# A gate computed inside an attention, and scatters issued beside it

## The reference

```python
x = x + attention(layernorm(x), ctx, mask)          # 16 heads of 16, 77 keys
xn = layernorm(x)
scores = softmax(xn @ Wg)                           # Wg 256 x 32, 32 experts
weights, indices = top_k(scores, 4)
for e in range(32):                                 # capacity 2048 pairs each
    tok, w = the pairs that chose e, in order
    y[tok] += swiglu(xn[tok], W1[e], W2[e], W3[e]) * w
x = x + y + swiglu(xn, Ws1, Ws2, Ws3)               # shared expert, width 256
x = x + attention(layernorm(x), ctx)
x = x + ffn(layernorm(x))                           # weights of +1 and -1
```

## Time and profile before

| | |
|---|---|
| three runs | 1355.96 us median, 1355.4 to 1363.51 |
| the profiled execution | 1356.17 us; its span in the trace 1354.4 us |
| granted TensorE clock, mean | 0.933 |
| PE / DVE / ACT / POOL busy | 87% / 57% / 38% / 30% of the span |

### The profile page before, as it was taken

One profiled execution on the slowest core, in us unless ns is written; L12 is line 12 of the kernel. 1 busy time (PEld: TensorE's weight loads), 2 busy tenths in 40 slices (PEclk: granted clock), 3 DMA queues, 4 the chain that ended last, 5 costly groups with the idle time before them and its releaser, 6 DMA issues. The chain is left out here.

```text
span 1354.4 us, 26011 instructions
## 1 busy us (share of the span) xinstructions
PE 1172.3 (87%) x8528; PEld 810.8 (60%) x8528; DVE 765.4 (57%) x2032; ACT 512.3 (38%) x1049; POOL 409.5 (30%) x495
## 2 busy tenths in 40 slices
PE   7699999677682399999999448899989999999998
PEld 4378888445441277778877323788865555555554
DVE  4177778565562156666656495788873434244331
ACT  6555555222230034443433136566642222222221
POOL 5260000466575445555555344600000000000000
PEclk9899999787786799999999768899999999999999
DMA  9199100263162554445444291000000000000000
GB/s 176 24 308 392 49 2 2 82 102 95 66 216 101 190 163 148 148 147 180 152 136 118 90 371 51 14 2 2 1 2 1 16 16 17 0 15 15 16 16 16
DMA packets 100754, 123.94 MB, mean 92 GB/s; under 512 B 33984, under 2 KB 76051, under 8 KB 100631
## 3 DMA queue, kind: packets, MB, share of 16 engines
q1 hardware_dynamic: 86807, 87.98, 22.1%
q0 software_dynamic: 13824, 34.38, 7.1%
HBM read 61.78 MB, written 64.72 MB: 93 GB/s over the span
## 5 line engine op out<-in xcount | busy, mean ns | idle before, releaser
L1847 PE MATMUL psA<-H,B 128*128 128x512 f16 x1024 | 223.5, 379 | 0.0
L1774 DVE SCALAR_TENSOR_TENSOR H<-psA,H 128x512 f16<-128x512 f32 x128 | 88.3, 690 | 208.3 <-ACT H L1815 208.3
L1533 POOL DMA_INDIRECT y_rows<-YB,pair x160 | 155.5, 972 | 149.0 <-DVE YB L1588 80.9
L1815 ACT ACTIVATE H<-psA 128x512 f16<-128x512 f32 x128 | 76.4, 597 | 252.7 <-PE psA L1847 252.7
L1847 PEld LDWEIGHTS psA<-H,B 128*128 128x128 f16 x1024 | 100.2, 98 | 119.3
L1643 PE MATMUL psH<-W,XT 128*128 x640 | 168.1, 386 | 0.5 <-ACT XT L1545 0.4
L203 POOL TENSOR_SCALAR var<-mv 128x4 f32<-128x4 f32 x32 | 13.7, 429 | 508.2 <-DVE mv L197 507.1
L1206 POOL DMA_INDIRECT x_rows<-XN,slot_s x128 | 130.6, 1021 | 71.5 <-issue 43.9
L806 DVE TENSOR_TENSOR PLT<-psT,PHT 128x512 f16<-128x512 f32 (+1 forms) x192 | 113.9, 595 | 38.8 <-ACT PHT L857 38.3
L857 ACT ACTIVATE PHT<-psT 128x512 f16<-128x512 f32 (+1 forms) x192 | 94.4, 525 | 102.4 <-PE psT L916 102.4
L1643 PEld LDWEIGHTS psH<-W,XT 128*128 128x128 f32 x640 | 110.1, 192 | 12.0 <-issue 3.1
(11 more groups left out here) (249 smaller groups left out, 2039.0 us busy)
## 6 DMA issues: line engine op xcount, KB each, us to landing
XG<-x_rows SPq DMA_DIRECT2D x160, 134.0 KB
y_rows<-zero_row SPq DMA_DIRECT2D x4, 4096.0 KB, 27.5
G<-y_rows SPq DMA_DIRECT2D x7, 2048.0 KB, 10.3
x_rows<-zero_row SPq DMA_DIRECT2D x33, 134.0 KB, 8.7
X<-in_x SPq DMA_DIRECT2D x8, 512.0 KB, 7.2
QT<-in_w SPq DMA_DIRECT2D x1, 4096.0 KB
out_x<-OUT SPq DMA_DIRECT2D x8, 512.0 KB
y_rows<-YB,pair POOLq DMA_INDIRECT x160
```

The lines of the kernel that those rows point to most:

```text
L1533: pool.indirect_dma_start(y_rows[:, :], bass.IndirectOffsetOnAxis(ap=pair[u // HALF][:, u % HALF:u % HALF + 1], axis=0), YB[u][:], None, b ...
L1774: dve.scalar_tensor_tensor(out=H[layer][1][:, o], in0=psA[k % 4][:], scalar=0.0, in1=H[layer][0][:, o], op0=ALU.max, op1=ALU.subtract).the ...
L1847: last = pe.matmul(psA[k % 4][:], W[:, c, o * P:(o + 1) * P], src[part][:, c], start=n == 0, stop=n == 2 * n_in - 1)
```

## The change

A class `Gate` takes the place of `Chosen`, `RouteTail` and the gate code of route. Its steps are called from `body(t)` of the first attention, each at a slot `t = K + 4 m`: transposes at K = 8, logits at 9, pick and index at 11, mark at 12, ranks at 13, place and slots at 14; ACT's `apply` at 7 writes the normalized rows straight into the row buffers (before: DVE L210, then ACT L1370). The statistics of one tile are at the end of each body. `mark` is one comparison and two bf16 additions where there was a reduction (L1010). Six macros are gated there, a seventh is transposed there, and 70 of the 128 scatters are issued there: all 16 of macros 0 to 3, and 6 of macro 4. In route remain the gates of macros 6 and 7 (bodies 0 and 1) and 58 scatters; plan, second keys and values are at other bodies, w1 comes in attention, and W2 in 16 pieces of 256 KB behind the `up`s.

```diff
-ROWBUFS = 2
+ROWBUFS = 4
+GATED_EARLY, SCATTERED_EARLY, TURNED_EARLY = 6, 4, 7
+CUT = 6
+TURN_AT, LOGITS_AT, PICK_AT, RANKS_AT, SCATTER_AT = 8, 9, 11, 13, 15
+KEYS_AT = 1
 # attend, gpsimd
+                    for m in range(SCATTERED_EARLY):
+                        gate.scatter(pool, m, 0, MT * TOPK)
+                        gate.power(pool, m + MT - 1)
+                    gate.scatter(pool, SCATTERED_EARLY, 0, CUT)
 # attend, vector: body(t)
+                    if gate:
+                        for m in gate.due(t, RANKS_AT + 1, GATED_EARLY):
+                            dve.wait_ge(gate.c_done, m + 1)
                     if ok(t - 2):
                         norm(t - 2, u)
+                    if gate:
+                        gate_reads(t)
                     if ok(t + 1):
                         maximum(t + 1, 1 - u, 0)
...
+                    if gate:
+                        gate_steps(t)
 # attend, scalar: end of body(t)
...
+                        for m in gate.due(t, LOGITS_AT + 1, GATED_EARLY):
+                            gate.exps(act, m)
+                        for h in range(2):
+                            for m in gate.due(t, TURN_AT, TURNED_EARLY):
+                                gate.turned_out(act, m, h, rows_piece(m, h))
+                            for m in gate.due(t, TURN_AT - 1, TURNED_EARLY):
+                                gate.apply(act, m, h)
+                        for m in gate.due(t, PICK_AT + 1, GATED_EARLY):
+                            gate.tops(act, m)
 # attend, tensor: body(t)
+                        for m in gate.due(t, TURN_AT, TURNED_EARLY):
+                            for h in range(2):
+                                bank_free(pe, (gate, m, h))
+                                gate.turn(pe, m, h, rows_piece(m, h))
+                        for m in gate.due(t, RANKS_AT + 1, GATED_EARLY):
+                            pe.wait_ge(gate.ranks_read, m + 1)
                     if ok(t - 1):
                         values(t - 1, 1 - u)
...
+                        for m in gate.due(t, RANKS_AT, GATED_EARLY):
+                            gate.ranks(pe, m)
+                        for m in gate.due(t, LOGITS_AT, GATED_EARLY):
+                            bank_free(pe, (gate, m, "logits"))
+                            gate.logits(pe, m, logits_piece(m))
 # Gate
+        def recycled(self, eng, m):
+            if m >= ROWBUFS:
+                eng.wait_ge(self.scattered[m % ROWBUFS], SCATTERS * (m // ROWBUFS))
...
+        def mark(self, dve, m):
...
+            self.own.done(dve.tensor_tensor(self.two, self.hot[:, :, 0:2, :], self.hot[:, :, 2:4, :], ALU.add))
+            dve.tensor_tensor(self.chosen, self.two[:, :, 0, :], self.two[:, :, 1, :], ALU.add).then_inc(self.chosen_s, 1)
 # route, sync
-                load_down(sp)
+                def down(m):
+                    sp.wait_ge(h_done, (m + 1) * 2 * KC)
+                    load_down(sp, 2 * m, 2)
+                    load_down(sp, EXPERTS // 2 + 2 * m, 2)
 # route, tensor
+                for b in range(MACROS):
+                    if b < PLAN_AT:
...
+                        gate.logits(pe, GATED[b], psL)
+                    up(b, 0)
+                    if b:
+                        shared_out(b - 1)
...
+                    up(b, 1)
...
```

More of the change, by code:

```diff
@@ L745, in ok @@
             return not isinstance(t, int) or 0 <= t < TILES
+        TURNS = []
+        for t in range(TILES + 3):
+            TURNS += [(t, g) for g in range(NG) if t < TILES]
+            if gate:
+                TURNS += [(gate, m, h) for m in gate.due(t, TURN_AT, TURNED_EARLY) for h in range(2)]
+                TURNS += [(gate, m, "logits") for m in gate.due(t, LOGITS_AT, GATED_EARLY)]
+        ORDER = {key: i for i, key in enumerate(TURNS)}
         def steady(body, beside):
@@ L1189, in _ @@
                         sp.dma_start(x_rows[ds(row, P), :], zero_row[:, 0:ROW]).then_inc(tails_st, 16)
+                for m in range(PLAN_AT, MACROS):
+                    down(m)
                 sp.wait_ge(tails_st, 16 * EXPERTS)
@@ L1211, in _ @@
-                for m in range(MACROS):
-                    body(m, m % ROWBUFS)
+                kv.blanks(pool)
+                gate.power(pool, MACROS - 1)
+                for m in range(SCATTERED_EARLY, MACROS):
+                    first = CUT if m == SCATTERED_EARLY else 0
+                    gate.scatter(pool, m, first, MT * TOPK)
                 for b in range(ROWBUFS):
-                    pool.wait_ge(scattered[b], SCATTERS * len(range(b, MACROS, ROWBUFS)))
+                    pool.wait_ge(gate.scattered[b], SCATTERS * len(range(b, MACROS, ROWBUFS)))
@@ new lines, in silu, with rest_out @@
+                    act.activation(SG[:, o], psH[bank(m, o, 0)][:], ACT.Silu).then_inc(silu_s, 1)
+                def rest_out(m):
+                    act.wait_ge(gate.turned, 2 * m + 2)
+                    act.activation(QT[:, :, m * MW:(m + 1) * MW], psX[:], ACT.Copy).then_inc(gate.xt_out, 2)
+                for m in range(TURNED_EARLY, MACROS):
+                    for h in range(2):
+                        gate.apply(act, m, h)
+                for b in range(MACROS):
+                    if b < PLAN_AT:
+                        gate.exps(act, GATED[b])
+                    silu(b, 0)
+                    if b < PLAN_AT:
+                        gate.tops(act, GATED[b])
+                    if b == KEYS_AT:
@@ L1464, in body @@
                                   stop=True).then_inc(plan_spread, 1)
-                    if m:
-                        shared_out(m - 1)
-                    if m + 2 < MACROS:
-                        turn_in(m + 2, u)
-                        logits(m + 2, u)
-                pe.sem_inc(turned, 1)
-                pe.sem_inc(l_done, 1)
-                ranks(0, 0)
-                turn_in(1, 1)
-                logits(1, 1)
-                for m in range(MACROS):
-                    body(m, m % 2)
+                    if b == KEYS_AT:
+                        pe.wait_ge(gate.l_shift, MACROS)
+                        kv.keys(pe)
                 shared_out(MACROS - 1)
```

654 lines of the change are left out of this document (339 added, 315 removed).

## The result

The changed kernel took 1387.34 us (median of four runs, 1380.79 to 1391.55), the kernel before 1357.53 beside it: a ratio of 1.0208, 95% interval 1.0155 to 1.0261. It is slower by 2.1%, where 1313 was forecast. The profiled execution took 1388.31 us, 32 more than the one before.

The account below looks back on a forecast made before the run. PE was taken to bound attention 1 and POOL's scatters to pace route. From 1356.2 us, route's -113, attention's +55 and unnamed waits' +15 gave 1313, with a range of 1274 to 1358.

Parts of the forecast that it names:

- What bounds route: Route before the change: paced by POOL's scatters and small operations, some 23 us a macro, 184 of 229 us.
- part 1: Route without its moved scatters and gates: PE becomes the bound, route falls from 229.1 to 116.4 us, a gain of 113.
- the 17 I added: Route, beyond PE's work: 8.0 us for the slow clock at its beginning, 3.5 for three bubbles, 6 for start and end.
- Part 2: Attention 1 with the gate's work: 9.2 us more a macro, +55 us in all, lower bound +30.
- 0.25 us of room behind the lows: Attention's tile: DVE work behind the last low or before the maximum hides only about 0.25 us, then lengthens the path.
- my 2.8: Attention, tiles t = 13 and 14: ranks and logits on PE, shift and place on DVE, cost 2.8 us.
- Rival B: Attention: DVE's gate steps fall into its idle time, +30 instead of +55; 1288, or 1273 with no unnamed wait; chance 0.17.
- Part 3: Waits with no named releaser (51 us in route before) seem to need back-to-back scatters: +15 us, bounds 0 and 51.
- D: Attention and route: an unbroken run of scatters holds DVE and ACT until it ends; 1377 us, chance 0.12.
- its 79 us of waits: Held time in the slower rival: 30 us for attention's five runs, 43 for route's row of 42 scatters, 6 more there.
- as many per scatter as before: Upper bound for unnamed waits over the 128 scatters: 51 us, 0.4 each.
- The port lock: Attention: GpSimd's scatter descriptors wait out DVE's maxima, scatters every 2.8 us, attention ends at 340; 1354 us, chance 0.03.

Follow-up runs that it names:

- quiet occasion: Condition shared by all kernels of one comparison: the kernel before takes 1305 to 1308 us; the changed kernel, unaltered, took 1248.11 us (0.9576).
- holding: Condition shared by all kernels of one comparison: the kernel before takes 1348 to 1358 us; the changed kernel, unaltered, took 1387.34 and 1388.36 us.
- version with pairs: Changed kernel with a small GpSimd operation after every second attention scatter and route's scatters spread: 1285.93 us (0.9487 of kernel before) holding, 1265.26 (0.9663) quiet.

## Why the prediction was wrong

- **What bounds route, and part 1: right.** With 40 us for some 54 of added GpSimd time its pace is borne out. Route came to 104.2 us on a quiet occasion, against 116 forecast: its PE work is 100.2 busy us as summed (98.9), at a clock of 0.95, so the bubbles and the start cost less than the 17 I added. W2's pieces and the plan were hidden, and the seam fell to under 4 us.
- **Part 2, +55: mis-sized.** It is +36 on a quiet occasion. The mechanism held (a macro's four tiles take 26.8 us instead of 20.3), but what I took as 0.25 us of room behind the lows was up to 1 us, as much as the two gaps of 0.70 and 0.29 in the earlier trace rows together, which are gone in the first two of these tiles: 1.6 to 2.3 us of DVE work there cost 1.2 to 1.4 a tile, and only the tile with place ahead of the maxima came near my 2.8, at 2.6. Rival B's size was nearer. The timeline of DVE on the quiet occasion, one pair of maxima to a tile, shows 6.5, 6.3, 6.3 and 7.7 us where the earlier trace rows have 5.07:

```profile
148.51 1.51 DVE L848 TENSOR_REDUCE mx<-psS 128x8 fp32r<-128x616 f32 x2
...
155.00 1.49 DVE L848 TENSOR_REDUCE mx<-psS 128x8 fp32r<-128x616 f32 x2
...
161.28 1.50 DVE L848 TENSOR_REDUCE mx<-psS 128x8 fp32r<-128x616 f32 x2
...
167.60 1.51 DVE L848 TENSOR_REDUCE mx<-psS 128x8 fp32r<-128x616 f32 x2 [0.56 <-PE psS L981]
...
175.27 1.51 DVE L848 TENSOR_REDUCE mx<-psS 128x8 fp32r<-128x616 f32 x2
```

- **Part 3, +15 for the unnamed waits: this step failed.** It should have been 121 in this comparison: 79.8 us in attention and 41.3 in route over the same program on a quiet occasion. (Experts' 19 are in the kernel before as well and cancel.) The sum with the measured terms is 1356.2 - 125 + 36 + 121 = 1388, where the execution took 1388.31. "The row nearest to attention's pace is that of experts" was the error: I compared mean rates, and the mean did not matter. Attention's scatters come back to back with a rest behind sixteen, as route's did, and the nearest row was the 23.97 us in the earlier trace rows. The trace of before held more: the ranks for which DVE L1239 waits until 432.98 were done on PE at 406.73, 26 us earlier, in the middle of an unbroken run of scatters from 389.83 to 429.74.

```profile
406.48 0.25 PE L1434 MATMUL psR<-chosen,ones_b 128*128 128x32 bf16 x4
```

The 51 us over 128 scatters were also no price per scatter: route's work has little that PE must signal, so most of a run went by unnoticed there, while a tile of attention hands over between PE, DVE and ACT many times and stands still (this last is argued from the order of the work, not measured). That waits are not a price shows in the totals too: of the 40 to 50 us between the kernel before in the two conditions experts makes 19, so the 51 us of waits cost its route some 20 to 30 (an estimate; its route has no quiet trace without pauses).
- **The rival that came true was D**, given 0.12, with its mechanism and nearly its time (1377 for 1387). That the time came so near was partly luck: its 79 us of waits were 42 too few, and the sum it shares with the forecast 31 too many (19 in part 2, 12 in part 1). Its point of decision was wrong: not 14 us into a run but from the third or fourth scatter. Its 6 us for each run in attention were 18 to 19 (a macro lasts 45 us, and 27 on a quiet occasion), its 49 in route 41. The bound "as many per scatter as before" was taken for the worst case though the trace held a worse one.
- **The port lock did not show.** No row had shown that the maxima, which read psS, would hold the port. Scatters in attention kept a median of 0.97 us beside a DVE that was 61% busy, and 83% on the quiet occasion, so they waited for no maxima; attention of the quiet occasion ended at 277.5, not at 340.
- **What could not be read from one trace** is that the condition differs. The range of 1274 to 1358 covers neither kind: quiet it is 1248, holding 1387. Set against the kernel before of the same occasion the forecast of -43 lies between -57 and +30.

The two kernels compare as follows: on a quiet occasion the changed one is 4.2% faster, on a holding one 2 to 3% slower. The version with pairs beats the kernel before on both (0.949 and 0.966), and the changed kernel where signals are held (1286 against 1388, from two holding occasions), at the price of 17 us where they are not (1265 against 1248, from two quiet occasions).

## What to carry to other kernels

Before you move a long row of back-to-back scatters beside a stage in which engines hand over to each other every microsecond, look for waits without a named releaser near such rows in the old place, and compare the producer's end with the consumer's start there: the stage that hides late signals now need not be the one that gets them. A pause after every second scatter can be tried at once; here it cost 17 us on a quiet occasion and gave 100 on a holding one. Measure such a change on more than one occasion: here its sign changed between two. And compare rows by how the events come (in a row or apart), not by their mean rate.

## What the runs showed of the hardware

- Under the holding condition a row of GpSimd's indirect DMAs delays what PE signals (by 14 to 17 us in the place shown; 26 us in route of the kernel before) and slows what it issues (a matmul of `shared_out` each 2.1 or 2.8 us instead of 0.22); DVE's signal to PE in the same place took 0.05 us. Plain DMAs of the same rows from the same queue did not do it (attention 216.4 us instead of 295.8). By what mechanism a row of scatters does it was not found.
- Experts is longer under that condition in every kernel (284 to 298 us against 270 to 272 in the traces read), with scatters of 972 ns in both. This was not followed up.
- What makes an occasion holding or quiet stayed open. Three comparisons were holding and four quiet, each without exception for all the kernels in it; the devices numbered 0 and 15 were met in both conditions, so it does not go with the chip.
